# A two-layer cross-attention kernel on one core: five batches in flight instead of three, one one-hot with row-moved keys and values, and small work moved between VectorE, ScalarE and GpSimd

## The chip, the cores and the metric

The kernel runs on one NeuronCore of a Trainium2 chip. The metric is the device time of one execution in microseconds (us). The profile's engines are PE (TensorE matmuls; PEld is its weight loads), DVE (VectorE), ACT (ScalarE), POOL (GpSimd) and SP (SyncE, which issues DMAs).

## What is computed

Sixteen batches of 512 tokens, width 256, with 64 context rows for each batch. Layer 0 lets each token attend to the three context rows at its index minus one, its index, and its index plus one (where they exist), in 16 heads. Layer 1 attends to all 64 rows through a softmax and ends in a LayerNorm. Cut to what matters:

```python
# layer 0, x: (16, 512, 256), ctx: (16, 64, 256), idx: (16, 512)
q = split(rmsnorm(x, gq) @ Wq0.T); kn = rmsnorm(ctx, gkv); k = split(kn @ Wk0.T); v = split(kn @ Wv0.T)
mask = abs(arange(64) - idx[:, :, None]) <= 1
w = where(mask, square(relu(q @ k.T / sqrt(16))), 0)
out = (w / maximum(w.sum(-1, keepdims=True), 1e-6)) @ v
x = x + out @ Wo0.T
# layer 1
q = gelu(x @ Wq1 + bq); k = gelu(ctx @ Wk1 + bk); v = gelu(ctx @ Wv1 + bv)
x1 = softmax(q @ k.T) @ v @ Wf + bf + x
return layernorm(x1) * ln_gamma + ln_beta
```

## The kernel before, in words

Tokens are picked by matmul. For a batch, VectorE compares the token indices (L796, `build_onehot`) with three constants and gets three one-hot matrices `onehot[:, s, :]`, one for each neighbour s. TensorE multiplies the layer-0 keys `kv0[:, f, 0, :]` by each one-hot (L388, `picked_keys`) and so has for every token the key row of its neighbour s in PSUM. VectorE multiplies these by the queries `q0` (L819, `multiply_keys`); a matmul with a selector (L495) sums them by head; ScalarE applies Relu (L702), TensorE turns the sums to token rows (L513), ScalarE squares them (L709) into `w`, and VectorE makes the normalised weights `wn` (L883 to L892). The values are picked in the same way (L394, `picked_values`), and VectorE multiplies them by `wn` into `att[:, s]` (L870, `attend`). TensorE then turns the three `att[:, s]` into column form and adds them in PSUM at the same time: three times 8 transposes of 128x128 (L414, `turn`). ScalarE and VectorE split the result into a high and a low part (`o_hi` L733, `o_lo` L927), since every projection is done as three products of float32r parts (L346 to L348, `product`).

The output projection is added to x (L861, `xpT`), split again (L687 `xp_hi`, L864 `xp_lo`), projected (`queries1`) and put through Gelu (L722). The 64 scores per token come from L562; they are copied (`scT`, L726), turned to rows (L570), and VectorE takes the row maximum (L912), subtracts it (L914, `sdiff`), ScalarE takes the exponential (L728), and VectorE sums it (L919), inverts (L921) and scales it (L923, `enf`). TensorE turns this (L580), ScalarE copies it (L736, `eT`), and the product with the final values (L465, called z here) is added in PSUM to x, which was turned into it (L550). VectorE takes the statistics (`bn_stats`, L834) and works out the variance in six instructions of 128x4 (L839 to L846); GpSimd raises it to the power -1/2 (L310) and makes the bias (L313); ScalarE normalises in four instructions (L666); GpSimd multiplies by gamma (L321), adds beta (L323) and issues the store (L325). GpSimd also makes `x_lo` (L298) for a coming batch.

All of this is written out by hand for every engine, with semaphores. One turn of the loop works on three batches: f in layer 0, b = f-1 in the first part of layer 1 and n = f-2 at its end (`steps`, L167; VectorE runs it in two halves, `steps_turned`, L176). Each engine runs its own list strictly in order. The prologue makes keys and values of all batches; `kv0` is filled partly by SP's DMAs (`cross`).

Of the kernel before, what the change touches and what calls it, by code (L numbers as in the profile page):

```python
# [19 lines left out]
C_ID, C_SEL, C_POS, C_EPS, C_END = 0, 128, 224, 227, 228  # L20


def xattn_pair(nc: bass.Bass, xT, ctx, ctxT, idx, vectors, wq0T, wk0T, wv0T, wo0T,
# [9 lines left out]
    with es:  # L33
# [10 lines left out]
        pos = [cst[:, C_POS + s:C_POS + s + 1] for s in range(SHIFTS)]  # L44
# [41 lines left out]
        sdiff = sb("sdiff", [P, TT, K])  # L86
        ex = sb("ex", [P, TT, K])
# [16 lines left out]
        def rows(t):  # L104
# [3 lines left out]
        ctxT_sb = qkp[:, 4:6, :]  # L108
# [13 lines left out]
        w = ps[:, 4, 0:SHIFTS * TT * H].rearrange("p (s j h) -> p s j h", s=SHIFTS, j=TT)  # L122
# [39 lines left out]

        FIRST_STEADY, LAST_STEADY = 2, B - 1

        def steps(engine, step):  # L167
            step(0, None, None)
            step(1, 0, None)
            for i in range(FIRST_STEADY, LAST_STEADY):  # L170
                step(i, i - 1, i - 2)
            step(B - 1, B - 2, B - 3, last=True)
            step(None, B - 1, B - 2)
            step(None, None, B - 1)

        def steps_turned(engine, head, tail):  # L176


            head(0, None, None)
# [22 lines left out]

        K1_BANKS = (2, 3, 6, 7)
        KV_BANKS = (6, 7, 2, 3)
        crossing = [kv_cross[:, 0, :, :], kv_cross[:, 1, :, :], w_hi["o0"][:, :, :], w_lo["o0"][:, :, :],
                    w_hi["q1"][:, :, :], w_lo["q1"][:, :, :], kv_cross[:, 0, :, :], kv_cross[:, 1, :, :]]
        V1_BANKS = (2, 3)

        @block.sync
        def _(sp):  # L210
# [22 lines left out]

            context_columns(0)
# [747 lines left out]
```

## Time and profile before

| | us |
|---|---|
| median of 3 runs | 406.25 (405.65 to 407.63) |
| profiled execution, its own time | 407.22 |
| its span in the profile | 405.4 |
| PE busy | 370.7 (91%) |
| DVE busy | 306.2 (76%) |
| ACT busy | 231.6 (57%) |
| POOL busy | 148.8 (37%) |

The span begins with the first and ends with the last instruction on the core; the execution's own time is 1.8 us longer. Busy PE is not PE at its peak, since matmuls are pipelined; the gap between the starts of two matmuls is the better price of one.

### The profile page before, as it was taken

The numbers are of one execution on the slowest core, as the hardware profiler recorded it, in microseconds if no ns is written. First come the engines' busy times: TensorE is split into PE (matmuls) and PEld (weight loads), VectorE is DVE, ScalarE is ACT, GpSimd is POOL, SyncE is SP. The second block draws the span as 40 slices with busy tenths as digits, with TensorE's granted clock in tenths as the row PEclk, the third lists the DMA queues.
The fourth block names the chain that finished last, engine by engine and source line by source line (L and its number), as shares of the span: only waits on it lengthen the run. The fifth ranks groups of instructions, "written<-read, shape, count | busy, mean of one in ns | idle before, by whom it ended". The sixth has DMA issues, their size and how long they took to land.

```text
span 405.4 us, 5734 instructions
## 1 busy us (share of the span) xinstructions
PE 370.7 (91%) x2132; PEld 262.5 (65%) x2132; DVE 306.2 (76%) x588; ACT 231.6 (57%) x379; POOL 148.8 (37%) x102
## 2 busy tenths in 40 slices
PE   3977999999999999999999999999999999998660
PEld 1653886858576776767676767676768576756540
DVE  0888266887979796969696969697978879797614
ACT  4793413557475656575656657474747474746441
POOL 0630002035353534434343525253535353515151
PEclk9998999999999999999999999999999999999985
DMA  8875056012011212121212121212121110010111
GB/s 253 282 214 158 0 128 159 0 54 64 32 72 43 78 53 78 53 79 54 78 54 78 53 78 53 78 52 81 52 77 54 41 68 25 0 53 11 41 53 52
DMA packets 17339, 30.24 MB, mean 75 GB/s; under 512 B 1568, under 2 KB 7712, under 8 KB 17312
## 3 DMA queue, kind: packets, MB, share of 16 engines
q1 hardware_dynamic: 14192, 21.22, 17.3%
q0 software_dynamic: 2160, 7.87, 5.5%
q10 hardware_dynamic: 960, 0.79, 0.6%
q8 instruction: 17, 0.28, 0.3%
q14 instruction: 10, 0.08, 0.1%
HBM read 17.29 MB, written 8.39 MB: 63 GB/s over the span
## 4 chain that ended last, share of the span: by engine, by line
PE 80%; issue 7%; ACT 5%; DVE 4%; POOL 3%; ACTq 0%; POOLq 0%; DVEq 0%
PE ps L346 11%; PE ps L348 10%; PE ps L347 10%; PE ps L414 10%; PE ps L495 7%; PE ps L394 7%; PE ps L388 6%; PE ps L465 4%; PE ps L562 4%; PE ps L550 3%; PE ps L513 2%; PE ps L378 2%; PE ps L580 1%; PE ps L570 1%; POOL crs L294 1%
## 5 line engine op out<-in xcount | busy, mean ns | idle before, releaser
L298 POOL TENSOR_TENSOR x_lo<-x_ring,x_hi 128x1024 fp32r<-128x1024 f32 x16 | 38.4, 2401 | 104.5 <-ACT x_hi L642 104.5
L666 ACT ACTIVATE bufs<-ps,nbias,rstd 128x256 f32<-128x256 f32 x64 | 32.3, 561 | 65.6 <-issue 55.6
L321 POOL TENSOR_TENSOR bufs<-bufs,lng_row 128x1024 f32<-128x1024 f32 x15 | 35.9, 2396 | 87.5 <-ACT bufs L666 87.5
L870 DVE TENSOR_TENSOR qkp<-ps,wn 128x1024 f32<-128x1024 f32 x48 | 57.3, 1221 | 6.2 <-PE ps L394 4.9
L819 DVE TENSOR_TENSOR qkp<-ps,bufs 128x1024 f32<-128x1024 f32 x48 | 57.1, 1217 | 0.1
L414 PE MATMUL ps<-cst,qkp 128*128 128x128 f32 x384 | 50.3, 275 | 0.0
L414 PEld LDWEIGHTS ps<-cst,qkp 128*128 128x128 f32 x384 | 42.5, 140 | 5.9 <-DVE qkp L870 5.8
L388 PE MATMUL ps<-onehot,kv 128*128 128x512 f32 x96 | 33.9, 436 | 6.5 <-issue 4.8
L323 POOL TENSOR_TENSOR bufs<-bufs,lnb_row 128x1024 f32<-128x1024 f32 x15 | 35.7, 2378 | 1.2
L883 DVE TENSOR_REDUCE den<-ps 128x64 f32<-128x192 f32 x16 | 5.7, 358 | 40.2 <-ACT ps L709 40.2
L495 PE MATMUL ps<-qkp,cst 128*32 128x512 f32 x192 | 32.0, 621 | 2.2 <-DVE qkp L819 2.2
L394 PE MATMUL ps<-kv,onehot 128*128 128x256 f32 x192 | 33.1, 299 | 0.2 <-DVE wn L892 0.2
L394 PEld LDWEIGHTS ps<-kv,onehot 128*128 128x128 f32 x192 | 27.0, 189 | 9.4 <-ACT bufs L666 5.2
L495 PE MATMUL ps<-bufs,cst 128*32 128x512 f32 x64 | 31.8, 621 | 0.0
L310 POOL TENSOR_TENSOR rstd<-var,minus_half 128x4 f32<-128x4 f32 x16 | 16.5, 1029 | 37.3 <-DVE var L846 37.3
L864 DVE TENSOR_TENSOR xp_lo<-bufs,xp_hi 128x512 fp32r<-128x512 f32 x32 | 20.9, 689 | 10.1 <-ACT xp_hi L687 10.0
L346 PE MATMUL ps<-xp_hi,wh_q 128*128 128x512 f32 x64 | 26.4, 412 | 2.3 <-DVE xp_lo L864 2.3
L722 ACT ACTIVATE bufs<-ps,vec 128x512 f32<-128x512 f32 x32 | 22.1, 690 | 9.3 <-PE ps L348 9.1
L346 PE MATMUL ps<-x_hi,wh_q 128*128 128x512 f32 x64 | 27.1, 423 | 0.0
L388 PEld LDWEIGHTS ps<-onehot,kv 128*128 128x128 f32 x96 | 14.5, 189 | 18.1 <-issue 15.1
L834 DVE BATCH_NORM_STATS2 stats<-ps 128x6 f32<-128x256 f32 x64 | 22.7, 419 | 4.4 <-PE ps L465 4.4
L348 PE MATMUL ps<-xp_lo,wh_q 128*128 128x512 f32 x64 | 25.3, 395 | 0.0
(137 smaller groups left out, 831.7 us busy)
## 6 DMA issues: line engine op xcount, KB each, us to landing
x_ring<-xT SPq DMA_DIRECT2D x16, 512.0 KB, 3.5
out<-bufs POOLq DMA_DIRECT2D x15, 512.0 KB, 3.4
idx_ring<-idx SPq DMA_DIRECT2D x16, 256.0 KB, 3.7
vfd<-bufs SPq DMA_DIRECT2D x8, 256.0 KB, 5.3
qkp<-ctxT SPq DMA_DIRECT2D x2, 512.0 KB, 7.5
bufs<-ctx SPq DMA_DIRECT2D x2, 512.0 KB, 8.9
kv<-kv_cross SPq DMA_DIRECT2D x8, 128.0 KB, 2.4
out<-bufs SPq DMA_DIRECT2D x2, 256.0 KB, 2.2
```

Of the source, the lines that this page charges most:

```text
L298: G.tensor_tensor(x_lo[:, :, :], x_ring[:, f % RING, :, :], f32_view(x_hi[:, :, :]), ALU.subtract).then_inc(xl_ready, 2)
L321: G.tensor_tensor(zo, zn, lng_row[:, :].unsqueeze(1).broadcast_to([P, TT, D]), ALU.mult).then_inc(zg_ready, 1)
L323: G.tensor_tensor(zo, zo, lnb_row[:, :].unsqueeze(1).broadcast_to([P, TT, D]), ALU.add).then_inc(zo_ready, 1)
L346: mm(o, hi, m_hi, start=start, stop=False)
L347: mm(o, lo, m_hi, start=False, stop=False)
L348: last = mm(o, hi, m_lo, start=False, stop=stop)
L388: i = mm(ps[:, bank0 + g, :], kv0[:, f, 0, g * P:(g + 1) * P], onehot[:, s, :], start=True, stop=True)
L394: i = mm(ps[:, bank0 + j // 2, (j % 2) * D:(j % 2 + 1) * D], onehot[:, s, j * P:(j + 1) * P], kv0[:, f, 1, :], start=True, stop=True)
L414: i = mm(ps[:, g, j * P:(j + 1) * P], att[:, s, j, g * P:(g + 1) * P], ident, is_transpose=True, start=(s == 0 and j == 0), stop=(s == SHI ...
L495: i = mm(ps[32 * s:32 * s + 32, 4, :], sum_sel[:, g if s < SHIFTS else 2, :], qk[:, s, g, :] if s < SHIFTS else xsq[:, g, :], start=(g == ...
L819: V.tensor_tensor(qk[:, s, :, :], ps[:, bank0:bank0 + 2, :], q0, ALU.mult).then_inc(qk_ready, 1)
L870: V.tensor_tensor(att[:, s, :, :].rearrange("p j (h d) -> p (j h) d", d=HD), ps[:, bank0:bank0 + 2, :].rearrange("p a (h d) -> p (a h) d", ...
```

## The change

Both kernels compute the same function. What is different:

- **One turn of the loop holds five batches.** `step(e, a, f, b, n)` for step s works on e = s (split of x), a = s-1 (queries, picked keys, head sums), f = s-2 (weights, picked values), b = s-3 (sum over the neighbours, output projection, layer-1 queries and scores) and n = s-4 (softmax, z, LayerNorm). Every engine's list is written in a new order, and the PSUM banks are given out anew.
- **One one-hot.** It compares with `pos` = row, and is kept for two batches. The neighbours come from copies of the keys and values moved up and down by one row (`kvs`), which SP makes with four SBUF-to-SBUF DMAs of 63 rows per batch (`shifted`); GpSimd clears the two buffers once (`clear_shifted`).
- **VectorE adds the three neighbours** (two additions of 128x1024), and TensorE turns only the sum: 8 transposes instead of 24. Two of the three `attend` products are written into PSUM in place.
- **Softmax:** VectorE negates the row maximum (128x4), and ScalarE takes the exponential in four instructions with the maximum as a bias and the row sum as accumulated output. `sdiff` and `ssum` on VectorE are gone.
- **LayerNorm:** the six small instructions leave VectorE; GpSimd does the whole chain in ten small instructions.
- GpSimd multiplies and adds gamma and beta before it makes `x_lo`; before, `x_lo` came first. The last batch waits for all four normalised tiles before VectorE finishes it.

```diff
+            for s in range(1, B + 4):
+                e, a, f, b, n = (i if 0 <= i < B else None for i in (s, s - 1, s - 2, s - 3, s - 4))
+                step(e, a, f, b, n)
...
+            def shifted(i):
...
+                if i > 1:
+                    sp.wait_ge(kvs_in[r], 64 * (i // 2))
+                    sp.wait_ge(vg_mm, 3 * (i - 2) + 2)
+                for lo in (0, K):
+                    sp.dma_start(f32_view(kvs[r][lo:lo + K - 1, 0, :, :]), f32_view(kv0[lo + 1:lo + K, i, :, :])).then_inc(kvs_in[r], 16)
+                    sp.dma_start(f32_view(kvs[r][lo + 1:lo + K, 1, :, :]), f32_view(kv0[lo:lo + K - 1, i, :, :])).then_inc(kvs_in[r], 16)
...
-            def turn(f, s, groups=range(DC)):
-
-                pe.wait_ge(att_ready, 3 * f + s + 1)
-                for g in groups:
-                    for j in range(TT):
-                        i = mm(ps[:, g, j * P:(j + 1) * P], att[:, s, j, g * P:(g + 1) * P], ident,
-                               is_transpose=True, start=(s == 0 and j == 0), stop=(s == SHIFTS - 1), skip_group_check=True)
...
+                    pe.wait_ge(sum_ready, 2 * b + 2)
+                    for g in range(DC):
+                        for j in range(TT):
+                            i = nc.tensor.transpose(ps[:, TURN_BANKS[g], j * P:(j + 1) * P], att[:, 0, j, g * P:(g + 1) * P], ident)
+                        i.then_inc(o_mm, 1)
...
+                if a is not None:
+                    if n is not None:
+                        pe.wait_ge(zn_ready, 2 * n + 2)
+                    up_keys(a)
...
+                if n is not None:
+                    act.wait_ge(nmax_ready, n + 1)
+                    for j in range(TT):
+                        A(ex[:, j, :], sc_rows[:, j, :], ACT.Exp, bias=nmax[:, j:j + 1],
+                          accum_out=ssum[:, j:j + 1]).then_inc(ex_ready, 1)
...
+                if n is not None:
+                    normalise(range(2, TT))
+                if a is not None and f is not None:
...
+                    copy_q0(a, 1)
+                if n is not None:
+                    normalise(range(0, 2))
```

The places on which the prediction rests, as each engine's list has them. VectorE (DVE) in the softmax of one batch, before: `attend` (L870), three one-hots (L796), the maximum, the subtraction, the row sum, its inverse and `enf` (`qkp` holds `qk` and `att`, `bufs` holds `q0`).

```order
L870 TENSOR_TENSOR qkp<-ps,wn 128x1024 [waits vg_mm] x2
L796 TENSOR_SCALAR onehot<-idx_ring,cst 128x512 [waits vg_mm,idx_in]
L796 TENSOR_SCALAR onehot<-idx_ring,cst 128x512
L912 TENSOR_REDUCE smax<-ps 128x4 [waits sc_mm]
L914 TENSOR_TENSOR sdiff<-ps,smax 128x256 [waits smax_ready]
L796 TENSOR_SCALAR onehot<-idx_ring,cst 128x512 [waits vg_mm,idx_in]
L919 TENSOR_REDUCE ssum<-ex 128x4 [waits ex_ready]
L921 RECIPROCAL rsum<-ssum 128x4 [waits ssum_ready]
L923 TENSOR_TENSOR enf<-ex,rsum 128x256 [waits rsum_ready]
```

The subtraction, the row sum and two of the one-hots leave this engine.

The same engine after, from the last `multiply_keys` (L845) over `attend` of the centre (L856), the maximum and its negative, the addition that ends batch b (L883), to the inverse of the softmax sum. One-hot work is one instruction, and `nmax` and the sum now stand here.

```order
L845 TENSOR_TENSOR qkp<-ps,bufs 128x1024 [waits kg_mm,s_mm,q0_cp]
L845 TENSOR_TENSOR qkp<-ps,bufs 128x1024 [waits kg_mm] x2
L856 TENSOR_TENSOR ps<-ps,wn 128x1024 [waits vg_mm]
L954 TENSOR_REDUCE smax<-ps 128x4 [waits sc_mm]
L956 TENSOR_SCALAR nmax<-smax 128x4 [waits smax_ready]
L883 TENSOR_TENSOR qkp<-ps,qkp 128x1024 [waits sum_ready,att_ready]
L886 RECIPROCAL rsum<-ssum 128x4 [waits ex_ready]
```

The maximum has moved from ahead of `o_lo` to ahead of the sum on which the next step's transposes wait.

GpSimd (POOL) before, one whole turn of its loop.

```order
L298 TENSOR_TENSOR x_lo<-x_ring,x_hi 128x1024 [waits xh_ready]
L310 TENSOR_TENSOR rstd<-var,minus_half 128x4 [waits var_ready]
L313 TENSOR_TENSOR nbias<-nmean,rstd 128x4 [waits nmean_ready,rstd_ready]
L321 TENSOR_TENSOR bufs<-bufs,lng_row 128x1024 [waits out_done,zn_ready]
L323 TENSOR_TENSOR bufs<-bufs,lnb_row 128x1024 [waits zg_ready]
L325 DMA out<-bufs 128x4x256 [waits zo_ready]
```

Here `x_lo` is done before the statistics of the batch come in.

GpSimd after, one turn without the first of its ten small instructions (`mean_gap`, L328): they stand ahead of the gamma and beta work, and `x_lo` (L315) comes behind it.

```order
L329 TENSOR_TENSOR m2_sum<-stats 128x4
L331 TENSOR_TENSOR gap_sq<-mean_gap 128x4 [waits gap_ready]
L333 TENSOR_SCALAR m2_part<-m2_sum 128x4 [waits parts_ready]
L334 TENSOR_TENSOR mean2<-stats 128x4
L337 TENSOR_TENSOR var4<-m2_part,gap_sq 128x4 [waits var_ready,gap_ready]
L339 TENSOR_SCALAR nmean2<-mean2 128x4 [waits mean_ready]
L341 TENSOR_TENSOR half_rstd<-var4,minus_half 128x4 [waits var_ready]
L344 TENSOR_TENSOR rstd<-half_rstd 128x4 [waits mean_ready,rstd_ready]
L345 TENSOR_TENSOR nbias<-nmean2,half_rstd 128x4
L353 TENSOR_TENSOR bufs<-bufs,lng_row 128x1024 [waits out_done,zn_ready]
L355 TENSOR_TENSOR bufs<-bufs,lnb_row 128x1024 [waits zg_ready]
L315 TENSOR_TENSOR x_lo<-x_ring,x_hi 128x1024 [waits xh_ready]
```

The power and the bias are no longer the first that GpSimd does for a batch, and `x_lo` now waits for ScalarE's normalised tiles too, through the order of the list.

TensorE (PE) after, from the head sums (L459) over the next step's start to `queries0` (L381): the 8 transposes (L510) wait for VectorE's sum, those of the head sums (L515) for ScalarE's Relu, those of the softmax (L520) for `enf`. Before, the 24 transposes stood between other matmuls.

```order
L459 MATMUL ps<-qkp,cst 32x512 [waits xsq_ready,qk_ready]
L459 MATMUL ps<-qkp,cst 32x512 x2
L459 MATMUL ps<-bufs,cst 32x512
L459 MATMUL ps<-qkp,cst 32x512 x3
L459 MATMUL ps<-bufs,cst 32x512
L510 MATMUL ps<-cst,qkp 128x128 [waits sum_ready]
L510 MATMUL ps<-cst,qkp 128x128 x7
L515 MATMUL ps<-cst,s_sb 128x128 [waits s_cp]
L515 MATMUL ps<-cst,s_sb 128x128 x3
L520 MATMUL ps<-cst,enf 128x128 [waits enf_ready]
L520 MATMUL ps<-cst,enf 128x128
L381 MATMUL ps<-x_hi,wh_q0 128x512 [waits xl_ready,xh_ready]
```

Three waits on other engines now stand one behind the other at the start of a step.

## Rows read from the trace of the kernel before

**Rows 1.** The page: busy time, share of the span and instructions of each engine.

```profile
PE 370.7 (91%) x2132; PEld 262.5 (65%) x2132; DVE 306.2 (76%) x588; ACT 231.6 (57%) x379; POOL 148.8 (37%) x102
```

**Rows 2.** Timeline of PE, the L465 groups: start us, us, engine, operation, idle before.

```profile
82.41 1.14 PE L465 MATMUL ps<-vfd,eT 64*128 64x256 f32 x8
...
358.43 1.13 PE L465 MATMUL ps<-vfd,eT 64*128 64x256 f32 x8
...
377.64 1.14 PE L465 MATMUL ps<-vfd,eT 64*128 64x256 f32 x8 [0.81 <-DVE o_lo L927]
...
393.20 2.08 PE L465 MATMUL ps<-vfd,eT 64*128 64x256 f32 x8 [0.47 <-ACT eT L736]
```

**Rows 3.** Windows: one step, busy time (and count) of each engine in it.

```profile
221.26:242.50 21.24, 20.89 (x128) 14.96 (x127) 17.48 (x35) 13.07 (x22) 9.23 (x7) 1.00 0.18 62
```

**Rows 4.** Chain that ended last, window 221.26 to 242.5: shares by line, longest pieces.

```profile
by line: PE ps L346 13.9%; PE ps L414 13.0%; PE ps L347 13.0%; PE ps L348 13.0%; PE ps L394 10.2%; PE ps L495 8.7%; PE ps L388 8.6%; PE ps L465 5.0%; PE ps L562 4.8%; PE ps L550 4.1%; PE ps L513 2.1%; PE ps L580 1.8%; issue 1.7%; PE ps L570
...
226.62 1.75 PE ps L414 x16
```

**Rows 5.** Groups by line, VectorE, whole run: count, busy us and mean ns, idle before.

```profile
L870 DVE TENSOR_TENSOR qkp<-ps,wn 128x1024 f32<-128x1024 f32 x48 | 57.3, 1221 | 6.2 <-PE ps L394 4.9
L819 DVE TENSOR_TENSOR qkp<-ps,bufs 128x1024 f32<-128x1024 f32 x48 | 57.1, 1217 | 0.1
L796 DVE TENSOR_SCALAR onehot<-idx_ring,cst 128x512 fp32r<-128x512 int32 x48 | 24.2, 535 | 0.0
L834 DVE BATCH_NORM_STATS2 stats<-ps 128x6 f32<-128x256 f32 x64 | 22.7, 419 | 4.4 <-PE ps L465 4.4
...
L914 DVE TENSOR_TENSOR sdiff<-ps,smax 128x256 f32<-128x256 f32 x16 | 6.8, 424 | 0.5
L919 DVE TENSOR_REDUCE ssum<-ex 128x4 f32<-128x256 f32 x16 | 6.7, 421 | 2.2 <-ACT ex L728 1.0
...
L839 DVE TENSOR_TENSOR mean_gap<-stats 128x4 f32<-128x4 f32 x16 | 2.7, 166 | 0.5
```

**Rows 6.** Timeline of POOL, 220 to 243 us.

```profile
223.46 2.38 POOL L323 TENSOR_TENSOR bufs<-bufs,lnb_row 128x1024 f32<-128x1024 f32 x1
...
231.13 2.37 POOL L298 TENSOR_TENSOR x_lo<-x_ring,x_hi 128x1024 fp32r<-128x1024 f32 x1 [4.17 <-ACT x_hi L642]
234.73 1.03 POOL L310 TENSOR_TENSOR rstd<-var,minus_half 128x4 f32<-128x4 f32 x1 [1.23 <-DVE var L846]
235.84 0.20 POOL L313 TENSOR_TENSOR nbias<-nmean,rstd 128x4 f32<-128x4 f32 x1
```

**Rows 7.** Timeline of ACT, 220 to 243 us.

```profile
236.12 1.02 ACT L666 ACTIVATE bufs<-ps,nbias,rstd 128x256 f32<-128x256 f32 x2 [4.20 <-issue]
...
238.86 0.69 ACT L702 ACTIVATE s_sb<-ps,cst 128x512 f32<-128x512 f32 x1 [0.68 <-PE ps L495]
239.44 0.59 ACT L656 ACTIVATE bufs<-ps 128x512 f32<-128x512 f32 x1
```

**Rows 8.** Timeline of ACT in the prologue: squares with an accumulated sum.

```profile
8.33 0.42 ACT L611 ACTIVATE scT<-bufs 128x256 f32<-128x256 f32 x1 [1.37 <-DMA bufs<-ctx]
8.65 0.19 ACT L611 ACTIVATION_READ_ACCUMULATOR scT<-bufs 128x1 f32 x1
8.87 0.42 ACT L611 ACTIVATE scT<-bufs 128x256 f32<-128x256 f32 x1
```

**Rows 9.** Timeline of DVE, 220 to 243 us: the one-hots.

```profile
225.42 1.10 DVE L796 TENSOR_SCALAR onehot<-idx_ring,cst 128x512 fp32r<-128x512 int32 x2
...
227.45 0.48 DVE L796 TENSOR_SCALAR onehot<-idx_ring,cst 128x512 fp32r<-128x512 int32 x1
```

**Rows 10.** Timelines of DVE and of POOL in the prologue.

```profile
20.97 1.23 DVE L748 TENSOR_TENSOR xp_lo<-qkp,xp_hi 128x1024 fp32r<-128x1024 f32 x1
...
10.55 0.35 POOL L291 TENSOR_SCALAR cmean<-cms 128x4 f32<-128x4 f32 x1 [9.72 <-ACT scT L611]
...
21.11 1.14 POOL L291 TENSOR_SCALAR cmean<-cms 128x4 f32<-128x4 f32 x1 [3.40 <-ACT scT L611]
```

More of the change, by code:

```diff
@@ L497, in step @@
[L497 to L518 removed]
+                    pe.wait_ge(wn_ready, f + 1)
@@ L538, in step @@
+                if a is not None:
+                    pe.wait_ge(q0_cp, 2 * a + 2)
                 if b is not None:
                     queries1(1)
-                if f is not None:
-                    pe.wait_ge(att_ready, 3 * f + 1)
-                    picked_values(f, 2, 6)
-                    if first(f):
-                        for pair in range(2, 4):
-                            pe.wait_ge(vf_copied, pair - 1)
-                            final_values(pair)
-                def back(j):
-                    for c in range(DC):
-                        mm(out_rows(j, c * P, P), xpT[:, c, j * P:(j + 1) * P], ident,
-                           is_transpose=True, start=(j % 2 == 0 and c == 0), stop=False, skip_group_check=True)
@@ L699, in step @@
                 if f is not None:
                     act.wait_ge(s_mm, f + 1)
-                    A(s_sb[:, :], ps[:, 4, :], ACT.Relu, bias=den_eps).then_inc(s_cp, 1)
-                    if not last:
-                        copy_q0(f + 1, 0)
-                    if first(f):
-                        for e in range(DC):
-                            copy_values1(0, e)
-                    act.wait_ge(sT_mm, f + 1)
-                    A(w.rearrange("p s j h -> p j s h"),
-                      ps[:, 5, :].rearrange("p (j s h) -> p j s h", j=TT, h=32)[:, :, 0:SHIFTS, 0:H], ACT.Square).then_inc(w_ready, 1)
@@ L711, in step @@
-                    if first(f):
-                        copy_q0(1, 1)
-                        for e in range(DC):
-                            copy_values1(1, e)
+                    A(s_sb[:, :], ps[:, 0, :], ACT.Relu, bias=den_eps).then_inc(s_cp, 1)
+                if b is not None:
+                    for g in range(DC):
+                        act.wait_ge(o_mm, 2 * b + g + 1)
+                        A(o_hi[:, g, :], ps[:, TURN_BANKS[g], :], ACT.Copy).then_inc(oh_ready, 1)
+                if f is not None:
+                    act.wait_ge(sT_mm, f + 1)
+                    by_row = w.rearrange("p s j h -> p j s h")
+                    A(by_row, by_row, ACT.Square).then_inc(w_ready, 1)
@@ L715, in step @@
                 if n is not None:
                     normalise(range(2, TT))
-                if b is not None:
-                    for e in range(DC):
-                        if e == 1 and f is not None and not last:
-                            copy_q0(f + 1, 1)
-                        act.wait_ge(q1_mm, 2 * b + e + 1)
-                        i = A(q1T[:, e, :], ps[:, 2 + e, :], ACT.Gelu, bias=vec[:, 2, e:e + 1])
-                    i.then_inc(q1_ready, 1)
+                if a is not None and f is not None:
+                    if f == 0:
+                        for i in range(DC):
+                            copy_values1(1, i)
+                    copy_q0(a, 1)
@@ L924, in tail @@
-                if f is not None:
-                    for g in range(DC):
-                        dve.wait_ge(oh_ready, 2 * f + g + 1)
-                        V.tensor_tensor(o_lo[:, g, :], ps[:, g, :], f32_view(o_hi[:, g, :]), ALU.subtract).then_inc(ol_ready, 1)
-            steps_turned(dve, head, tail)
+                    V.tensor_scalar(nmax[:, :], smax[:, :], -1.0, None, ALU.mult).then_inc(nmax_ready, 1)
+            steps(step)
             dve.wait_ge(ln_in, 16 * 2)
```

704 lines of the change are left out of this document (365 added, 339 removed).

## The prediction

> **What bounds the kernel now.** I read the page first: TensorE is busy 91% of the span, VectorE 76% [rows 1]. Then the same landmark in every turn of the loop, the start of z (L465): 82.41 us for batch 0, 358.43 us for batch 13 [rows 2]. That is 13 turns in 276.02 us, 21.23 us each, and 129.4 us for everything else (82.4 ahead, 47.0 behind). One turn in the windows view: 21.24 us, PE busy 20.89, DVE 17.48, ACT 13.07, POOL 9.23, granted clock 1.00, the 2.4 GHz level [rows 3]. The chain of waits in that turn never leaves TensorE's lines except for 1.7% "issue" [rows 4]. So TensorE's list, end to end, is the length of a turn, and whatever else is idle costs nothing. The shares of the chain are also TensorE's prices, since they count start to start: of 21.24 us, L414 has 13.0% or 2.76 us for 24 transposes (16 of them take 1.75 us), the three lines of `product` 39.9% or 8.47 us for 36 (0.235 each), L394 0.72 us for each of three shifts, L388 0.61, L495 1.85, L465 1.06, L562 1.02, L550 0.87, L513 0.45, L580 0.38 [rows 4].
>
> **The change part by part.** *TensorE.* 16 transposes go: 16 x 0.11 = 1.8 to 1.9 us of a turn. The count of picked keys and values, products and the rest stays. If the small issue wait (0.36) goes too, TensorE alone could turn in 21.24 - 1.88 - 0.36 = 19.0 us.
>
> *VectorE.* It loses two one-hots (2 x 0.54), the subtraction (0.42), the row sum (0.42) and six 128x4 instructions (0.16 each, less where they overlap; I take 0.9) [rows 5]: 2.8 us. It gains two additions of 128x1024, nowhere shown; the nearest are L819 and L870, one PSUM and one SBUF input, 1.22 each [rows 5], so 2.4 us, and a 128x4 negation, 0.16. Two `attend` products write PSUM; no VectorE row does, so they may cost less or more than 1.22. I keep 1.22, bounded by 1.0 and 1.4, which in two instructions is under 0.5 us. VectorE ends near 17.3 busy. It does not bound by sum; its place in the chain counts.
>
> *ScalarE.* One exponential of 256 columns becomes four of 64 with accumulated sums. The squares in the prologue show what an accumulated output does: a second instruction of 0.19 follows, and 256 columns come every 0.54 us [rows 8]. 64 columns must take less; I take 0.46 each (bounds 0.35 and 0.54), 1.85 in all.
>
> *GpSimd.* The statistics chain becomes ten instructions. The power is 1.03 and the bias 0.20, starting 0.08 after it [rows 6]. Nine small ones at 0.20 to 0.28 and the power give 2.8 to 3.6; I take 3.5. If each `tensor_scalar` costs the 0.35 of L291 [rows 10] it is 3.8.
>
> *SP* gets four DMAs of 63 rows per batch; they wait for the values of two batches earlier and are used a turn later, so some 10 us of cover lies over them. The load of x on the same queue waits for nothing later than before. I cost them at nothing; if one came late it would stop `up_keys`.
>
> *The new order* is where time can be lost. I followed one turn from the first transpose (time 0). The exponentials wait for the negated maximum, which VectorE makes just ahead of its last addition (1.22), so they start at -1.3 and end at 0.55; ScalarE's Relu (0.69 [rows 7]) stands behind them, so the head-sum transposes start at 1.35, where TensorE had been free at 0.9. Then 0.45 + 0.38 + 6 x 0.235 + 1.06: z ends at 4.65. Statistics take 1.42 (22.7 us over 16 [rows 5]); GpSimd 3.5; ScalarE two tiles (1.02), `copy_q0` (0.59), two tiles (1.02) [rows 7], with overlap 2.5. Only then may TensorE run `up_keys`, whose banks hold z: that is at 12.4 with four handoffs of 0.1, while its own list would have reached it near 11.7. From there 0.61 + 1.41 + 0.61 + 0.72 + 1.02 + 0.87 + 0.38 + 1.85 = 7.5 us, or about 7.1 without the waits that those shares hold. VectorE's maximum, negation and addition (0.42 + 0.16 + 1.22 and handoffs) just fit beside the 1.85 us of head sums. Sum: 4.65 + 1.42 + 3.5 + 2.5 + 7.1 + 0.5 = 19.7 us. So the wait taken off by fewer transposes is partly given back by a ring through GpSimd and ScalarE. Bounds: 18.9 (TensorE alone) and 20.7 (slow small instructions, sums at 0.54).
>
> *Outside the 13 turns.* The first z now stands 4.65 into its step instead of near 1, with about the same work ahead: +3. The end: the step between z of 13 and 14 has 16 transposes less (-1.4 after its waits), but the last batch meets four exponentials for one (+1.4), the longer GpSimd chain (+1.5, since VectorE's six took 0.7 and the rest 1.3), and all four tiles before VectorE's last four instructions (+1.6): +3.1. 129.4 + 6.1 = 135.5.
>
> Sum: 135.5 + 13 x 19.7 = 391.6 us of span, and 1.8 around it: 393.4 us against 407.2 for the profiled execution (which itself is 0.2% above the median of 406.25). I say 393.
>
> **A hold between GpSimd and VectorE.** In the prologue the same GpSimd instruction L291 takes 0.35 us once and 1.14 us the second time, when it starts at 21.11 under VectorE's L748, which reads two SBUF inputs until 22.20; it ends 0.05 later [rows 10]. And of a pair of one-hots that starts at 225.42, while GpSimd's L323 runs until 225.84, the pair takes 1.10 us where one alone takes 0.48 [rows 6, 9]. So some VectorE instructions and GpSimd's exclude each other. After the change the negation of the maximum (SBUF to SBUF, 128x4) becomes ready about 5.9 us after the normalised tiles, and GpSimd is then in its third long instruction: 2.38 + 2.38 + 2.37 and gaps of 0.1 end at 7.3. The Trainium skill ("SBUF — State Buffer", section "Who interferes with whom") says that a `tensor_scalar` in a two-port mode and any GpSimd instruction hold the pair of ports for the whole instruction, and by it the negation would wait; the rows agree for the one-hot. No row shows it for four columns. By the sum without a hold the turn is 19.7, by the one with it 21.2.
>
> **Rivals.**
> 1. *The hold decides* (slower). Turn = 4.65 + 1.42 + 3.5 + 2.5 + 0.3 up to the tiles, then 7.3 + 0.16 + 1.22 + 0.1 = 21.2. It hits the 12 turns in which GpSimd still makes `x_lo`: 135.5 + 12 x 21.2 + 19.7 + 1.8 = 411 us, 1.0% slower. It decides as soon as the negation is ready before `x_lo` ends. For it: rows 6, 9 and 10. Against it: four columns may not go in the mode in which 512 do, and the hold seen cost only part of the overlap. Chance 0.28, between 406 and 416.
> 2. *TensorE's list stays the bound*: GpSimd's small instructions at 0.20 or under hide the ring. 18.9 a turn: 135.5 + 245.7 + 1.8 = 383. For it: VectorE's own small ones overlap. Against: each GpSimd one waits on a semaphore of the one before. Chance 0.12.
> 3. *The chain on GpSimd is longer*, without a hold on the negation: `xp_lo` (two SBUF inputs) runs just when the power ends, and each may wait for the other, up to 1 us: 20.6 a turn, 405 us. Chance 0.08.
> 4. *Both, or a late DMA*: over 416. Chance 0.08.
>
> **How the numbers follow.** The forecast (0.44) has 389 to 400 as its own range, from the bounds of the exponentials, the small instructions and the drain. The range over all cases, 382 to 413, leaves out rival 4, the upper end of rival 1 and part of rival 2, near 2 in 10. A measurement of this kernel tells about 0.5% from no change. Faster by more: 0.44 + 0.12 + half of rival 3 = 0.60. Within: 0.03 of rival 3 and the low end of rival 1, 0.08. Slower: 0.32.
>
> **What would show it.** Right: L510 has 8 transposes in a turn; the gap between two z starts is 19.7; TensorE waits about 0.4 ahead of the head-sum transposes on ScalarE's Relu and 0.7 ahead of `up_keys` on ScalarE's normalised tiles; GpSimd's ten take 3.5 from first to last. Wrong: if the negation of the maximum lasts 1.5 us and not 0.16 while GpSimd runs `x_lo`, rival 1 holds; if TensorE never waits before `up_keys`, rival 2; if `up_keys` waits for a DMA, rival 4; and if VectorE's products into PSUM stand at 1.6 or more, VectorE becomes the bound, which I have not priced.

## The result, and the profile after the change

The changed kernel takes 393.5 us (median of 4 runs, 391.1 to 395.9) where the kernel before took 405.95 in the same session (405.6 to 407.6): a ratio of 0.968, with a 95% interval of 0.963 to 0.974. The profiled execution took 392.2 us, its span is 390.4. The prediction was 393, in a range of 382 to 413. The number held. The account of a turn behind it did not: the prediction over-priced the chain through GpSimd and ScalarE and left out a hold of VectorE by GpSimd, by about the same amount, and the experiments below pull the two apart.

The page of the changed kernel, busy time by engine, answers to [rows 1]:

```profile
PE 335.9 (86%) x1876; PEld 236.8 (61%) x1876; DVE 324.4 (83%) x476; ACT 246.5 (63%) x491; POOL 182.3 (47%) x232
```

TensorE lost 34.8 us of busy time (370.7 to 335.9) and 256 instructions, the 16 transposes of 16 batches, but the span lost only 15.0 us. VectorE issues 112 instructions less and is nevertheless busy 18.2 us longer. That is the first thing to explain.

The timeline of PE at the first z (now L539) and at that of batch 13 answers to [rows 2]:

```profile
83.17 1.14 PE L539 MATMUL ps<-vfd,eT 64*128 64x256 f32 x8
...
341.80 1.14 PE L539 MATMUL ps<-vfd,eT 64*128 64x256 f32 x8 [0.60 <-ACT eT L747]
```

(341.80 - 83.17) / 13 = 19.9 us a turn, and 390.4 - 258.6 = 131.8 us for the rest. One turn in the windows view, with the columns of [rows 3]:

```profile
200.31:220.35 20.04, 18.58 (x110) 13.27 (x110) 18.74 (x27) 13.93 (x30) 11.03 (x14) 1.00 0.28 92
```

A turn of 20.04 us holds 18.58 of TensorE, at a granted clock of 1.00. Before, 21.24 held 20.89. So TensorE now stands still for 1.5 us of that turn, and the groups by line say for what. These are the groups of PE and of ACT with their idle time and what ended it:

```profile
L510 PE MATMUL ps<-cst,qkp 128*128 128x128 f32 x128 | 17.5, 279 | 17.9 <-DVE qkp L883 17.9
L731 ACT ACTIVATE ps<-ps,nmax 128x64 f32<-128x64 f32 x64 | 18.3, 285 | 19.1 <-DVE nmax L956 19.1
```

The view of one tile, `nmax` (count, then shortest / median / longest in ns, first and last start):

```profile
L956 DVE TENSOR_SCALAR nmax<-smax x16: 170/1436/1476, 78.4 to 373.4; 128x4 f32<-128x4 f32 x16
```

The negation of four maxima per partition lasts 0.17 us at its shortest and 1.44 in the middle. Behind it on VectorE stands the sum L883, for which TensorE's transposes L510 wait; and ScalarE's exponentials L731 wait for the negation itself. The timeline of one turn, all four engines, shows what the negation waits for:

```profile
216.77 2.38 POOL L315 TENSOR_TENSOR x_lo<-x_ring,x_hi 128x1024 fp32r<-128x1024 f32 x1
...
217.24 0.42 DVE L954 TENSOR_REDUCE smax<-ps 128x4 f32<-128x256 f32 x1 [0.29 <-PE ps L624]
217.70 1.48 DVE L956 TENSOR_SCALAR nmax<-smax 128x4 f32<-128x4 f32 x1
219.09 1.21 DVE L883 TENSOR_TENSOR qkp<-ps,qkp 128x1024 f32<-128x1024 f32 x1
...
219.21 0.29 ACT L731 ACTIVATE ps<-ps,nmax 128x64 f32<-128x64 f32 x1 [1.52 <-DVE nmax L956]
219.42 0.19 ACT L731 ACTIVATION_READ_ACCUMULATOR ps<-ps,nmax 128x1 f32 x1
219.51 0.28 ACT L731 ACTIVATE ps<-ps,nmax 128x64 f32<-128x64 f32 x1
...
218.44 0.61 PE L459 MATMUL ps<-qkp,cst 128*32 128x512 f32 x3
...
220.35 1.09 PE L510 MATMUL ps<-cst,qkp 128*128 128x128 f32 x8 [1.30 <-DVE qkp L883]
221.28 0.60 PE L515 MATMUL ps<-cst,s_sb 128*128 128x128 f32 x4
```

GpSimd's x_lo ends at 219.15; the negation, ready at 217.70, ends at 219.18. TensorE is through with the head sums at 219.05 and starts the transposes at 220.35. Rival 1's mechanism is in plain sight. It also shows what hid it from the sum: the exponentials come every 0.29 us, not 0.46, and TensorE goes from L510 to the head-sum transposes L515 without the wait on Relu that the prediction had there.

### The profile page after: what moved, and what is told of

Read it like the earlier page. It is cut to its first block and busy times, and to the rows that moved or that the text cites. A ratio compares the mean times of both kernels' runs of the same rounds, so it can differ in the third digit from the quotient of the medians.

```text
span 390.4 us, 5504 instructions
## 1 busy us (share of the span) xinstructions
PE 335.9 (86%) x1876; PEld 236.8 (61%) x1876; DVE 324.4 (83%) x476; ACT 246.5 (63%) x491; POOL 182.3 (47%) x232
## 5 line engine op out<-in xcount | busy, mean ns | idle before, releaser
L315 POOL TENSOR_TENSOR x_lo<-x_ring,x_hi 128x1024 fp32r<-128x1024 f32 x16 | 38.7, 2416 | 41.0 <-ACT x_hi L687 41.0
L845 DVE TENSOR_TENSOR qkp<-ps,bufs 128x1024 f32<-128x1024 f32 x48 | 55.8, 1216 | 0.1
L758 ACT ACTIVATE xp_hi<-bufs 128x512 fp32r<-128x512 f32 x32 | 20.2, 632 | 54.7 <-DVE bufs L925 54.7
L328 POOL TENSOR_TENSOR mean_gap<-stats 128x4 f32<-128x4 f32 x16 | 3.1, 196 | 100.3 <-DVE stats L914 100.3
L856 DVE TENSOR_TENSOR ps<-ps,wn 128x1024 f32<-128x1024 f32 x32 | 39.2, 1225 | 2.8 <-PE ps L434 2.8
L510 PEld LDWEIGHTS ps<-cst,qkp 128*128 128x128 f32 x128 | 13.7, 140 | 31.8 <-DVE qkp L883 31.8
L510 PE MATMUL ps<-cst,qkp 128*128 128x128 f32 x128 | 17.5, 279 | 17.9 <-DVE qkp L883 17.9
L459 PE MATMUL ps<-qkp,cst 128*32 128x512 f32 x192 | 30.7, 598 | 1.9 <-DVE qkp L845 1.9
L459 PE MATMUL ps<-bufs,cst 128*32 128x512 f32 x64 | 30.5, 598 | 0.0
L381 PE MATMUL ps<-xp_hi,wh_q 128*128 128x512 f32 x64 | 26.9, 420 | 4.2 <-DVE xp_lo L928 4.2
L731 ACT ACTIVATE ps<-ps,nmax 128x64 f32<-128x64 f32 x64 | 18.3, 285 | 19.1 <-DVE nmax L956 19.1
L691 ACT ACTIVATE bufs<-ps 128x512 f32<-128x512 f32 x32 | 19.0, 597 | 14.5 <-PE ps L383 14.4
L381 PE MATMUL ps<-x_hi,wh_q 128*128 128x512 f32 x64 | 26.4, 413 | 0.0
L925 DVE TENSOR_TENSOR bufs<-ps,x_ring 128x512 f32<-128x512 f32 x32 | 21.9, 688 | 4.8 <-PE ps L383 4.8
L382 PE MATMUL ps<-xp_hi,wl_q 128*128 128x512 f32 x64 | 25.7, 402 | 0.0
L381 PE MATMUL ps<-o_hi,wh_o 128*128 128x512 f32 x64 | 25.2, 393 | 0.0
```

Of the source, the lines that this page charges most:

```text
L315: G.tensor_tensor(x_lo[:, :, :], x_ring[:, e % RING, :, :], f32_view(x_hi[:, :, :]), ALU.subtract).then_inc(xl_ready, 2)
L381: mm(o, hi, m_hi, start=start, stop=False)
L382: mm(o, lo, m_hi, start=False, stop=False)
L459: i = mm(ps[32 * s:32 * s + 32, 0, :], sum_sel[:, g if s < SHIFTS else 2, :], qk[:, s, g, :] if s < SHIFTS else xsq[:, g, :], start=(g == ...
L510: i = nc.tensor.transpose(ps[:, TURN_BANKS[g], j * P:(j + 1) * P], att[:, 0, j, g * P:(g + 1) * P], ident)
L845: V.tensor_tensor(qk[:, s, :, :], ps[:, bank0:bank0 + 2, :], q0, ALU.mult).then_inc(qk_ready, 1)
```

## The experiments

Each run is timed against the kernel before in its own session, where that one took 405.7 to 406.9 us. The turn is the usual distance of two z starts in the middle of the trace, 20.05 us in the changed kernel (19.9 is the mean over 13, whose last turn has no x_lo and lasts 18.08).

| kernel | median us | range | ratio to before (95%) | turn us |
|---|---|---|---|---|
| changed | 393.5 | 391.1 to 395.9 | 0.968 (0.963 to 0.974) | 20.05 |
| psum_max | 377.9 | 374.7 to 381.2 | 0.923 (0.916 to 0.931) | 18.79 |
| sum_first | 395.0 | 393.2 to 398.5 | 0.970 (0.963 to 0.977) | 19.97 |
| exp_one | 382.6 | 380.7 to 385.1 | 0.939 (0.933 to 0.945) | 19.05 |
| ln_dve | 395.2 | 394.0 to 397.2 | 0.970 (0.965 to 0.976) | 20.24 |
| psum_ln | 381.7 | 380.7 to 383.1 | 0.940 (0.936 to 0.943) | 18.96 |
| turns_x3 | 420.5 | 419.7 to 423.9 | 1.036 (1.031 to 1.042) | 21.84 |
| x_split | 379.9 | 378.2 to 382.8 | 0.935 (0.932 to 0.938) | 18.96 |
| neg_two | 391.7 | 390.3 to 395.0 | 0.965 (0.960 to 0.970) | 20.06 |
| neg_third | 377.7 | 374.9 to 378.4 | 0.928 (0.924 to 0.932) | 18.80 |
| neg_reduce | 374.5 | 373.6 to 381.6 | 0.922 (0.918 to 0.925) | 18.73 |

### psum_max: take the hold away by its operand

```diff
-        smax = sb("smax", [P, TT])
...
+        smax = ps[:, 4, 0:TT]
```

> The changed kernel, but VectorE writes the row maximum into four free PSUM columns of bank 4, so that the negation reads PSUM and writes SBUF; nothing else differs. Theory A (the hold): in the changed kernel the negation took 1.48 us because it could not run beside GpSimd's x_lo, and the sum behind it and TensorE's transposes behind that were late by as much. Then the negation drops to about 0.17 us, TensorE's wait ahead of the first transposes (1.30) goes to near nothing, the turn from 20.05 to 18.8 us, and the time by 12 x 1.25 = 15 us to about 379 us. Theory B (something else paces the turn, TensorE's own list or the ring through GpSimd and ScalarE, and the long negation only fills idle time): the negation shortens but the wait goes elsewhere, and the time stays within 2 us of 393.5. Theory C (the long negation is not a hold but the price of so small an instruction behind a reduction): it stays at 1.4 us and nothing changes.

The tile view of this kernel, then its timeline around the negation (VectorE and GpSimd), then one turn in the windows view:

```profile
L956 DVE TENSOR_SCALAR nmax<-ps x16: 161/162/163, 78.4 to 359.2; 128x4 f32<-128x4 f32 x16
```

```profile
209.40 0.43 DVE L954 TENSOR_REDUCE ps<-ps 128x4 f32<-128x256 f32 x1 [0.33 <-PE ps L624]
209.87 0.16 DVE L956 TENSOR_SCALAR nmax<-ps 128x4 f32<-128x4 f32 x1
209.95 1.23 DVE L883 TENSOR_TENSOR qkp<-ps,qkp 128x1024 f32<-128x1024 f32 x1
...
208.91 2.38 POOL L315 TENSOR_TENSOR x_lo<-x_ring,x_hi 128x1024 fp32r<-128x1024 f32 x1
```

```profile
198.16:217.01 18.85, 18.69 (x112) 13.30 (x111) 17.45 (x28) 13.97 (x28) 11.07 (x15) 1.00 0.27 99
```

The negation is 0.16 us in all 16 batches, in the middle of an x_lo of the same length. The time falls by 15.6 us, the turn by 1.26: theory A, to about a microsecond. VectorE is busy 309.0 us in this kernel, 15.4 less than in the changed one, so most of the 18.2 us to be explained was waiting in the hold.

TensorE is 18.69 us busy in 18.85, nearly without a pause. But the ring through GpSimd and ScalarE, to which the prediction gave 19.7 us, is still closed. The timelines of ScalarE, of TensorE's weight loads (PEld) and of its matmuls show the place ahead of `up_keys`:

```profile
202.98 1.03 ACT L724 ACTIVATE bufs<-ps,nbias,rstd 128x256 f32<-128x256 f32 x2
...
204.06 0.30 PEld L428 LDWEIGHTS ps<-onehot,wkv_lo 128*128 128x128 f32 x2 [0.59 <-ACT bufs L724]
...
203.51 0.40 PE L383 MATMUL ps<-xp_lo,wh_q 128*128 128x512 f32 x1
204.06 0.73 PE L428 MATMUL ps<-onehot,wkv_lo 128*128 128x512 f32 x2
```

The last normalised tile ends at 204.01 and `up_keys` starts at 204.06, 0.55 us behind the start of the matmul before it, where two such matmuls otherwise start 0.23 apart. So TensorE still gives up about 0.3 us there, and the turn is the ring: some 11.65 us from the first transposes to `up_keys` and 7.17 from there to the next ones make 18.8. TensorE's own list would turn in about 18.5, an estimate from these two figures (18.8 - 0.3).

### sum_first: which of the two victims counts

```diff
+                if f is not None:
+                    dve.wait_ge(att_ready, 3 * f + 3)
+                    dve.wait_ge(sum_ready, 2 * f + 1)
+                    V.tensor_tensor(att_flat(0), picked(2), att_flat(1), ALU.add).then_inc(sum_ready, 1)
                 if b is not None:
 
                     dve.wait_ge(sc_mm, b + 1)
                     V.tensor_reduce(smax[:, :], sc_rows, AX.X, ALU.max).then_inc(smax_ready, 1)
```

(and the same sum at the head of the step is gone)

> The changed kernel, but VectorE makes the last sum of a batch (1.21 us) ahead of the row maximum and its negation, not behind them. Theory A (hold): the sum ends at 218.2 instead of 220.3 on the clock of the turn that I read, the first transposes start when the head sums end (219.1), but the exponentials still start behind the held negation (219.2), Relu stands behind them, and the head-sum transposes wait for it: they come only 0.1 to 0.3 us earlier. So 12 x 0.2: about 391 us, 389.5 to 393. Theory B (only the sum's place matters, the exponentials have slack): the turn falls to 18.9 and the time to about 380. Theory C (the turn is paced elsewhere): 393 to 394.

The timeline, from VectorE, ScalarE and TensorE:

```profile
216.72 1.22 DVE L949 TENSOR_TENSOR qkp<-ps,qkp 128x1024 f32<-128x1024 f32 x1
217.86 0.41 DVE L953 TENSOR_REDUCE smax<-ps 128x4 f32<-128x256 f32 x1
218.31 0.61 DVE L955 TENSOR_SCALAR nmax<-smax 128x4 f32<-128x4 f32 x1
...
220.13 0.70 ACT L735 ACTIVATE s_sb<-ps,cst 128x512 f32<-128x512 f32 x1
...
218.73 1.10 PE L510 MATMUL ps<-cst,qkp 128*128 128x128 f32 x8
220.88 0.66 PE L515 MATMUL ps<-cst,s_sb 128*128 128x128 f32 x4 [1.05 <-ACT s_sb L735]
```

The transposes start right behind the head sums, as wanted, and the wait has moved one place on: 1.05 us ahead of L515, on a Relu that stands behind exponentials that stand behind the held negation (which again ends with x_lo, at 218.9). The turn is 0.08 us shorter. The hold has two victims, and saving one of them saves next to nothing. The median is 4 us above what was expected. 2.2 us of that is in the 13 turns, by the traces: 0.2 us is saved in all (258.63 to 258.44) and not 12 x 0.2, since the last of them, which has no x_lo, grew from 18.08 to 18.86. The other 1.8 lie outside them, where the drain varies from run to run (below).

### x_split: how long the hold lasts

```diff
-                G.tensor_tensor(x_lo[:, :, :], ...).then_inc(xl_ready, 2)
+                for c in range(DC):
+                    G.tensor_tensor(x_lo[:, c, :], ...).then_inc(xl_ready, 1)
```

> The changed kernel with GpSimd's x_lo (2.38 us) in two halves of 512 columns, so 1.2 us each. In the turn that I read x_lo ran from 216.77 to 219.15 and VectorE asked for the negation at 217.70. Theory A (the hold lasts as long as the GpSimd instruction that runs, and VectorE gets its turn between two): the negation is done near 218.1, the turn falls by about 1.0 us, 12 x 1.0 = 12: near 382 us. Theory B (GpSimd's next instruction is already queued and keeps the ports): no gain, 393 to 395 us. Theory C (no hold): no change either, but the negation stays at 1.48 us with its end away from an end of x_lo.

```profile
210.36 2.53 POOL L316 TENSOR_TENSOR x_lo<-x_ring,x_hi 128x512 fp32r<-128x512 f32 x2
...
211.31 0.36 DVE L957 TENSOR_SCALAR nmax<-smax 128x4 f32<-128x4 f32 x1
```

(timelines of POOL and DVE.) The negation is asked for at 211.31 under the first half and gets through near that half's end, 0.36 us after it was ready and not 1.45; the two halves together take 2.53 us instead of 2.38. The hold lasts as long as one running GpSimd instruction. The turn falls by 1.09 us with the same work on every engine.

### neg_two and neg_third: is it the form?

```diff
-V.tensor_scalar(nmax[:, :], smax[:, :], -1.0, None, ALU.mult)
+V.scalar_tensor_tensor(nmax[:, :], smax[:, :], -2.0, smax[:, :], ALU.mult, ALU.add)        # neg_two
+V.tensor_reduce(nmax[:, :], smax[:, :].unsqueeze(2), AX.X, ALU.max, negate=True)           # neg_third
```

> The changed kernel with the negation written in another form: a scalar_tensor_tensor that reads the maximum in SBUF twice (-2 x max + max) and writes SBUF, instead of a tensor_scalar with one input. It asks whether the form or the place of the operands makes the hold. Theory A (SBUF inputs make it, two of them as well as one): it is held in the same way, 1.4 to 1.5 us, and the time stays at 393.5, within 2. Theory B (only the form tensor_scalar is held): 0.17 us, and the time falls to about 379 us as with the maximum in PSUM.

> The changed kernel with the 128x4 negation as a tensor_reduce over one element with negation: one input in SBUF, output in SBUF, as the tensor_scalar has, and no other change. The tensor_scalar (one SBUF input) and the scalar_tensor_tensor (two SBUF inputs) were both held for 1.4 us. Theory A (SBUF in and out is what is held, whatever the form): 1.4 us again, 391 to 394 us. Theory B (with one SBUF input it is the form that decides, and a reduction does not take the shared ports; so the Trainium skill has it, SBUF — State Buffer, section Who interferes with whom): 0.17 to 0.2 us, and 378 us.

The tile view of each:

```profile
L956 DVE SCALAR_TENSOR_TENSOR nmax<-smax x16: 161/1458/1460, 77.4 to 372.5; 128x4 f32<-128x4 f32 x16
```

```profile
L956 DVE TENSOR_REDUCE nmax<-smax x16: 157/157/158, 77.5 to 356.1; 128x4 f32<-128x4 f32 x16
```

Two SBUF inputs are held just as one in a tensor_scalar is (1.46 us), a reduction with one SBUF input and an SBUF output is not (157 to 158 ns in all 16 batches). The first of these went as expected, the second against theory A, which had put the hold down to the place of the operands alone. It is place and form together. The Trainium skill ("SBUF — State Buffer", section "Who interferes with whom") names the same three cases: two SBUF inputs contend, a `tensor_scalar` in a two-port mode contends, a `tensor_reduce` never does. The runs agree in all three, though no trace shows the mode itself, and add that four columns are enough for the tensor_scalar.

### exp_one: undo the part on the exponentials

```diff
-A(ex[:, j, :], sc_rows[:, j, :], ACT.Exp, bias=nmax[:, j:j + 1], accum_out=ssum[:, j:j + 1])     # four times
+A(ex, sdiff[:, :, :], ACT.Exp)
...
-V.tensor_scalar(nmax[:, :], smax[:, :], -1.0, None, ALU.mult)
+V.tensor_tensor(sdiff[:, :, :], sc_rows, smax[:, :].unsqueeze(2).broadcast_to([P, TT, K]), ALU.subtract)
...
+V.tensor_reduce(ssum[:, :], ex, AX.X, ALU.add)
```

> The changed kernel with the part on the exponentials undone: VectorE subtracts the maximum from all 256 columns (reading PSUM and the SBUF maximum, writing SBUF), ScalarE takes one exponential of 256 columns, VectorE makes the row sums. No instruction of VectorE then reads and writes SBUF alone behind the maximum. Theory A (hold): the subtraction is not held (0.42 us), the sum of D1 ends 1.0 us earlier than before, ScalarE's Relu comes earlier as well, VectorE's list is 0.7 us longer; the turn goes to 18.9 to 19.3 us: 12 x 0.95 = 11 us faster than the changed kernel, about 382 us. Theory B (no hold at work; moving the sums to ScalarE was a gain): VectorE has 0.7 us more and is 83% busy already, so the turn grows by up to 0.5 us: 394 to 400 us.

The groups of DVE and PE:

```profile
L956 DVE TENSOR_TENSOR sdiff<-ps,smax 128x256 f32<-128x256 f32 x16 | 6.8, 425 | 0.6
...
L510 PE MATMUL ps<-cst,qkp 128*128 128x128 f32 x128 | 17.5, 280 | 6.2 <-DVE qkp L881 6.2
```

With 0.67 us more work on VectorE in every turn the kernel is 10.9 us faster than the changed one, because the subtraction (PSUM and SBUF in, 0.425 us) is not held. TensorE's wait ahead of L510 falls from 17.9 to 6.2 us. So as it was made, the part on the exponentials lost 11 us. Without a hold it is a gain: psum_max against exp_one is 4.7 us, 0.26 a turn.

### ln_dve and psum_ln: undo the part on GpSimd

```diff
 # VectorE, behind bn_stats: mean_gap, -(mean_e + mean_o), m2 sum, 0.25 gap^2, nmean, var
+V.scalar_tensor_tensor(gap_sq[:, :], mean_gap[:, :], 0.25, mean_gap[:, :], ALU.mult, ALU.mult)
...
 # GpSimd keeps
+G.tensor_tensor(rstd[:, :], var4[:, :], minus_half[:, 0:TT], ALU.pow)
+G.tensor_tensor(nbias[:, :], mean2[:, :], rstd[:, :], ALU.mult)
```

> The changed kernel with the part on the normalisation's small chain undone: six 128x4 instructions are back on VectorE, GpSimd keeps the power and one product. Theory A (hold; a turn is z's end 4.2 + statistics 1.4 + the chain 3.4 + tiles 2.4 + GpSimd's three long instructions 7.3 + the held sum 1.2): the chain falls from 3.4 to about 2.3 us, GpSimd's x_lo ends 1.1 us earlier in the turn and the negation with it. VectorE gets 0.9 us more, so that its own list of some 18.9 to 19.3 us comes up as the next bound. Turn 19.0 to 19.4, time 382 to 387 us, 385 likeliest. Theory B (VectorE's list is the bound now): +0.9 us in every turn, 404 us. Theory C (TensorE's list is the bound): no change, 393 us.

> The kernel with the maximum in PSUM (turn 18.85 us, 377.9 us), and with the normalisation's six small instructions back on VectorE and only the power and one product on GpSimd. It asks what moving the chain to GpSimd is worth when nothing is held. Theory A (TensorE's list is the bound of that kernel, and up_keys would wait only a little): with the six on VectorE the tiles were normalised 11.8 us after the turn's start instead of 11.6, so TensorE waits some 0.2 us ahead of up_keys: turn 19.0 to 19.1, time 380 to 382 us. Theory B (VectorE, 17.45 us busy in a turn of 18.85, is close enough that all 0.66 us of the six come through): turn 19.5, 387 us. Theory C (the shorter chain from statistics to bias, 2.2 instead of 3.4 us, is a gain): 376 or less.

ln_dve missed: 395.2 us where 385 was expected. The timelines of POOL and ACT in one turn of it (the transposes of that turn start at 201.67, those of the next at 221.91):

```profile
208.17 1.03 POOL L327 TENSOR_TENSOR rstd<-var,minus_half 128x4 f32<-128x4 f32 x1 [6.96 <-DVE var L910]
209.34 0.20 POOL L330 TENSOR_TENSOR nbias<-mean,rstd 128x4 f32<-128x4 f32 x1
...
209.88 1.23 ACT L743 ACTIVATE xp_hi<-bufs 128x512 fp32r<-128x512 f32 x2 [3.50 <-DVE bufs L920]
211.02 1.00 ACT L709 ACTIVATE bufs<-ps,nbias,rstd 128x256 f32<-128x256 f32 x2
```

The bias is ready at 209.54, 1.2 us earlier in its turn than in the changed kernel, but the tiles start at 211.02: ScalarE makes `xp_hi` first, and that waits for VectorE's L920, which stands behind the six small instructions. In the changed kernel `xp_hi` and the bias come within 0.2 us of each other (209.28 and 209.42), so the chain could not get shorter without VectorE's list getting shorter too. The expectation had followed only one of the two things that the tiles wait for. x_lo ends later, and the hold with it: 20.24 us a turn.

Without a hold (psum_ln) the part on GpSimd is worth 0.17 us a turn, and 3.8 us in the medians, of which the trace shows 2.8 in the 13 turns. It is a gain, and a small one. In psum_ln TensorE waits 0.4 us a turn ahead of `queries1` for VectorE's `xp_lo`, and hardly ahead of `up_keys`, where the expectation had put 0.2. `xp_lo` stands behind the six small instructions in VectorE's list.

### turns_x3: what the 16 transposes are worth

```diff
+                        for r in range(3):
                             for j in range(TT):
                                 i = nc.tensor.transpose(ps[:, TURN_BANKS[g], j * P:(j + 1) * P], ...)
```

> The changed kernel with the part on the transposes undone in TensorE's time alone: each of the 8 transposes of a batch is issued three times into the same place, so 24 as before the change, with VectorE's additions kept. Theory A (the transposes stand on the path: they wait for VectorE's last sum, everything after them waits for them, and the held negation is paced by what follows from z): 16 x 0.11 = 1.75 us in each of 16 steps, 28 us, so about 421 us. Theory B (ScalarE's exponentials and Relu end 0.2 us before the 8 transposes do, and TensorE has slack of 1.3 us a turn ahead of them, so a part is covered): +0.5 us a turn, 402 us.

27.0 us, 1.79 in a turn. Nothing of it is covered, in a kernel whose TensorE stands idle 1.3 us a turn: that idle time lies ahead of the transposes, and they wait for its end. With that TensorE time put back the changed kernel is 3.6% slower than the one before, so it was this part that made the change a gain.

### neg_reduce: the simplest version without a hold

```diff
-V.tensor_reduce(smax[:, :], sc_rows, AX.X, ALU.max)
-V.tensor_scalar(nmax[:, :], smax[:, :], -1.0, None, ALU.mult)
+V.tensor_reduce(nmax[:, :], sc_rows, AX.X, ALU.max, negate=True)
```

> The changed kernel with the negation inside the row maximum itself (the reduction negates its result), so that the 128x4 instruction is gone. It is meant as the simplest version without a hold. Theory A (hold, then TensorE's list as the bound at 18.85 us a turn): the same turn as with the maximum in PSUM, and one instruction and one handoff (0.2 us) less on the path of the last batches: 377 us, 374.5 to 379.5. Theory B (a turn of VectorE still matters at 18.85): 0.15 us a turn less, 375 us. Theory C (hold is not the cause): 391 to 394.

374.5 us, 7.8% under the kernel before and 4.8% under the changed one, with one instruction less. The turn is 18.73 us, and `up_keys` still waits for the tiles as in psum_max.

### The drain

Two kernels with the same turns can differ by some microseconds, and the windows view shows where. The two steps between the last three z starts and what is behind them, first of neg_reduce, then of sum_first (granted clock: the first figure behind the counts):

```profile
325.36:342.89 17.53, 12.10 (x72) 9.36 (x72) 13.13 (x23) 10.03 (x22) 9.00 (x13) 1.00 0.09 30
342.89:358.85 15.96, 9.81 (x52) 6.80 (x52) 5.63 (x12) 9.08 (x20) 8.23 (x13) 0.99 0.10 34
358.85:372.70 13.85, 2.08 (x8) 1.18 (x8) 4.10 (x8) 1.93 (x4) 2.58 (x10) 0.50 0.11 38
```

```profile
341.82:360.07 18.25, 13.91 (x72) 10.52 (x73) 13.59 (x24) 10.13 (x22) 9.00 (x13) 0.90 0.08 29
360.07:380.77 20.70, 14.48 (x52) 9.97 (x52) 5.53 (x13) 9.08 (x20) 8.16 (x13) 0.75 0.08 26
380.77:394.60 13.83, 2.08 (x8) 1.18 (x8) 4.11 (x8) 1.93 (x4) 2.58 (x10) 0.50 0.11 38
```

The same 52 TensorE instructions take 9.81 us at a granted clock of 0.99 (the 2.4 GHz level) and 14.48 at 0.75, a mix of both levels, and the step is 4.7 us longer. In the drain TensorE stands still for more than a third of the time even at the higher level, and the level differs from one trace to the next. The timed executions show the same: those of neg_reduce with a mean clock of 0.975 to 0.981 take 373.6 to 376.4 us, the one with 0.959 takes 381.6; sum_first takes 393.2 at 0.978 and 398.5 at 0.960. So differences under 2 us are read here from the turns and not from the medians.

## Why the prediction was right, and where it was not

**The bound of before and the price of the transposes: right.** 1.8 to 1.9 us a turn had been set for 16 transposes; turns_x3 measures 1.79. TensorE alone was to turn in 18.9 to 19.0; its own list would turn in about 18.5 (the estimate under psum_max), so that term was 0.5 too high, which did not count since the ring lies above it.

**"The new order ... 19.7 us": right in kind, too high by 1.0.** The failing step is the sum for the ring, and the turn of 18.73 to 18.79 us without a hold shows its size. It is not rival 2, though the time comes near rival 2's 18.9: by the prediction's own sign TensorE would then never wait ahead of `up_keys`, and it does. Term by term, from the first transposes of the turn at 200.31: z ends at 4.2 and not 4.65 (exponentials every 0.29 us, 1.17 in all and not 1.85, so Relu is done before the transposes are, where a wait of 0.45 had been put). Statistics 1.43 (1.42). GpSimd's ten 3.36 (3.5). Tiles 2.42 (2.5). The handoffs 0.2 in all (0.5). `up_keys` at 11.62 and not 12.4, behind a wait of 0.17 in the profile, or 0.3 by the gap between starts, and not 0.7; TensorE's own list would have reached it near 11.3 (11.7 had been said). The tail 7.1 (7.1). The largest error was the exponentials, 0.47 of the 0.97 us, whose price was taken between bounds of 0.35 and 0.54 and lay under the lower one: of [rows 8] the start-to-start 0.54 was scaled too timidly, from 256 columns to 64.

**The hold: priced rightly in kind, and given 0.28.** The prediction named the instruction, the partner and the sign by which to tell ("lasts 1.5 us and not 0.16": 1.44 to 1.48), and put it down as the less likely case since no row showed it for four columns. It was the case. By the working of rival 1 the turn was to be 21.2; it was 20.05, because the ring ahead of it was too high by 0.7 at the start of GpSimd's long instructions, and the rest by 0.4 (they took 7.2 us and not 7.3; the sum started under the end of the negation).

**Outside the turns: 135.5 predicted, 131.8 measured.** The first z is at 83.2 (85.4), and 48.6 follow the last of the 14 (50.1). The last step and the tail grew by 2.25 us where 4.5 had been put.

**How the number came out.** 393.4 - 13 x 0.97 (ring) - 3.7 (outside) + 15.2 (the hold, psum_max against changed over 13 turns) = 392.3, and the profiled execution took 392.2. A ring over-priced by 12.6 us and fixed parts by 3.7 cancelled a hold of 15.2 that had been left out. The direction was right for its main reason, the transposes; the size was right by accident. Had the prices been right, the same weighing would have given 377 as the forecast and 392 as rival 1.

**The costs that no row had shown held, but for one.** VectorE's products into PSUM (`attend`, L856) take 1.225 us, as into SBUF (1.22); its two sums 1.21 and 1.23 (1.22). No wait on the four DMAs of shifted rows appears on TensorE. GpSimd's `rstd` (L344) takes 0.73 us and not 0.20, held in turn by VectorE's xp_lo: the first half of rival 3, which costs at most 0.2 us a turn, because `xp_hi` (ready at 209.28, the bias at 209.42) is nearly as late.

**What stays open.** The new cyclic order was not tried apart from the other parts; the gains and losses given above are those of parts inside it. Of the 2.4 us between a turn of before and one of psum_max (21.24 and 18.85) the transposes are 1.79; of the other 0.6, the prediction had 0.36 for the issue wait of [rows 4], and no run takes it apart.

## What to carry to other kernels

When work moves to GpSimd, list the VectorE instructions that will run beside it and look at their operands: here one with two SBUF inputs, or a tensor_scalar from SBUF to SBUF, even of four columns, waited for the end of the GpSimd instruction, and everything queued behind it waited too. The cure costs next to nothing: an operand in PSUM, a reduction's own negation, or shorter GpSimd instructions, and here it gave 14 to 19 us, more than the 12.4 of the whole change. And a forecast that comes true should be checked term by term, since two errors can hide each other.

## What the runs showed of the hardware

- A 128x4 tensor_scalar from SBUF to SBUF waits for a running 128x1024 GpSimd tensor_tensor (1.44 us for 0.16), a scalar_tensor_tensor with two SBUF inputs as well (1.46), a tensor_reduce from SBUF to SBUF does not (0.157), nor does a tensor_scalar from PSUM to SBUF (0.162).
- The hold ends between two GpSimd instructions that follow each other without a gap: in x_split the median negation takes 0.36 us, and the two halves of x_lo 2.53 for 2.38.
- It goes both ways: GpSimd's 128x4 sum behind VectorE's xp_lo (two SBUF inputs) takes 0.73 us for 0.20.
- ScalarE's exponential of 128x64 out of PSUM with an accumulated sum comes every 0.29 us, the read of the accumulator included.
- In the drain the granted clock of the same step (52 or 53 TensorE instructions) was 0.75 to 1.00 from one trace to another, and the step up to 4.7 us longer.
